# Small attention heads issued unit by unit instead of pair by pair

## The reference

```python
q = (hidden @ Wq + bq).reshape(...)
scores = einsum(q, k) * scale + mask
attn = softmax(scores)
out = einsum(attn, v) @ Wo + bo
```

## Time and profile before

| | us |
|---|---|
| three runs | 1409.1, 1414.52, 1415.49 |
| median | 1414.52 |
| the profiled execution, its own time | 1412.02 |
| its span, first to last instruction | 1410.7 |
| layer 0 and its MLP, about | 0 to 719 |
| layer 1, stream of heads | 719 to 849 |
| layer 2, stream of heads | 916 to 1119 |
| layer 3, stream of heads, and the last batch's end | 1181 to 1410.7 |

### The profile page before, as it was taken

The page is one execution under the profiler, slowest core; times in us unless marked ns, Lnnn a source line. Parts: engine busy times, 40 slices in busy tenths (PEclk is TensorE's granted clock), DMA queues, the critical chain, the costliest instruction groups (busy, mean ns, idle before and its releaser), DMA issues. The chain is left out here.

```text
span 1410.7 us, 26853 instructions
## 1 busy us (share of the span) xinstructions
PE 1289.9 (91%) x9901; PEld 1098.9 (78%) x9901; DVE 903.1 (64%) x2341; ACT 721.6 (51%) x1817; POOL 547.4 (39%) x1003
## 2 busy tenths in 40 slices
PE   7999999999999999998977787978888898999995
PEld 6999999999999999997865556855554587666663
DVE  6866767688856767687765657455556375465661
ACT  4866666677756666576214443235444522444442
POOL 3544544445444545453443325043323131223332
PEclk9999999999999999999986889968997798899997
DMA  5320000023200000022012101220120112011000
GB/s 166 105 69 1 2 1 5 2 68 112 62 2 1 2 1 1 1 71 92 24 47 72 48 2 46 69 77 25 50 70 1 50 42 79 17 37 56 13 3 16
DMA packets 44132, 56.69 MB, mean 40 GB/s; under 512 B 10016, under 2 KB 24416, under 8 KB 44000
## 3 DMA queue, kind: packets, MB, share of 16 engines
q1 hardware_dynamic: 38880, 54.40, 12.3%
q0 software_dynamic: 5120, 0.56, 0.3%
HBM read 32.68 MB, written 1.05 MB: 24 GB/s over the span
## 5 line engine op out<-in xcount | busy, mean ns | idle before, releaser
L1797 ACT ACTIVATE PT<-bank 128x512 f32<-128x512 f32 x320 | 174.2, 595 | 165.5 <-PE bank L1739 84.2
L1078 POOL TENSOR_SCALAR E<-E,rl 128x256 f32<-128x256 f32 x256 | 238.1, 941 | 0.0
L1903 POOL DMA_DIRECT2D Q<-rows x160 | 90.3, 566 | 216.4 <-ACT rows L1811 208.5
L1076 POOL TENSOR_TENSOR pb<-E,rl 128x2 f32<-128x2 f32 x128 | 33.7, 263 | 327.4 <-DVE rl L954 327.4
L821 ACT ACTIVATE QTh<-bank,bqs 128x256 fp32r<-128x256 f32 x128 | 60.7, 474 | 182.6 <-PE bank L117 182.6
L1861 DVE CUSTOM_DVE_ANT_0 Em<-bank,M 128x256 bf16<-128x256 f32 x256 | 95.2, 420 | 75.7 <-issue 45.5
L1854 DVE TENSOR_REDUCE nm<-bank 128x1 f32<-128x512 f32 x128 | 82.3, 685 | 74.2 <-PE bank L1708 73.7
L831 ACT ACTIVATE E<-bank,nm 128x257 f32<-128x257 f32 x256 | 119.3, 480 | 3.1 <-DVE nm L931 3.1
L938 DVE SCALAR_TENSOR_TENSOR QTl<-bank,bqs,QTh 128x256 fp32r<-128x256 f32 x128 | 61.8, 483 | 85.3 <-ACT KT L822 84.4
L1754 PE MATMUL bank<-PT,V 128*32 128x256 f32 x1280 | 103.7, 462 | 2.6 <-ACT PT L1797 2.6
L1731 PE MATMUL bank<-Q,K 51*128 51x256 f32 (+1 forms) x640 | 97.4, 319 | 6.3 <-ACT PT L1797 5.4
(11 more groups left out here) (465 smaller groups left out, 4505.5 us busy)
## 6 DMA issues: line engine op xcount, KB each, us to landing
stage<-in_wts SPq DMA_DIRECT2D x99, 256.0 KB, 3.1
Q<-stage SPq DMA_DIRECT2D x72, 128.0 KB
K<-stage SPq DMA_DIRECT2D x48, 128.0 KB
K<-xh SPq DMA_DIRECT2D x16, 128.0 KB, 2.9
Q<-rows POOLq DMA_DIRECT2D x96, 4.0 KB, 1.7
K<-stage SPq DMA_DIRECT2D x24, 64.0 KB
X<-in_x SPq DMA_DIRECT2D x4, 256.0 KB, 6.0
stage<-in_ctx SPq DMA_DIRECT2D x4, 256.0 KB, 3.6
```

Of the source, the lines that this page charges most:

```text
L1078: m = pool.tensor_scalar(s.E[:, i % 3, t, 0:256], s.E[:, i % 3, t, 0:256], s.rl[:, r, t:t + 1], None, ALU.mult)
L1797: act.activation(s.PT[i % s.NPT][:, 2 * u:2 * u + 2, :].rearrange("p a b -> p (a b)"), s.STB[y][:], ACT.Exp).then_inc(S["t_ex"])
L1903: pool.dma_start(f32(s.Q[b % s.NR][at:at + 2, pair:pair + n, :]), f32(s.rows[4 * n * y:4 * n * y + 4 * n, g % 2, :])).then_inc(S[f"dma_row ...
```

## The change

The loop of all engines runs over units n instead of pairs: a unit is one bank of scores, that is one head in layers 1 and 3 and half a head in layer 2 (`TB` units a batch: 16, 32, 32). In step n TensorE issues the scores by query of unit n and the scores by key of unit n - L, with L odd (13, 17, 13), matmul by matmul in turn, so that one is always on the even head's rows and the other on the odd head's. Both waits, for the maximum of unit n - 2 and the exponential of unit n - L - 2, stand ahead of the step. In layer 3 the two mask matmuls follow each unit.

The projections `q`, `k`, `k1` (now `x`), `v0`, `v1` and `c` are cut in two pieces of six matmuls, each in a step of its own (`k` of layer 3 stays whole); high and low parts are steps of their own one unit apart (`qh`, `ql`, `th`, `tl`, ...). `q_out` in layer 1 comes at step 11 of 16, all outputs in layer 2 at step 15 of 32. An attend is cut in two halves, in two consecutive steps. The steps after attention and the norms for the next MLP get tables by unit (`POSTS`, `NEXT_NORMS`). `TURN` sets when a group's maxima are turned (1 to 2 units after they are complete). The number of `PT` buffers is 8, 6, 8 instead of 6. In layer 1 the maxima and exponentials per unit are as before; no arithmetic changes. In VectorE's and ScalarE's loops the preparations come before the unit's maximum or exponential.

```diff
-DELAY = {1: 6, 2: 4, 3: 5}
+TURN = {1: 2, 2: 3, 3: 2}
+LAG = {1: 13, 2: 17, 3: 13}
+KEPT = {1: 8, 2: 6, 3: 8}
...
+IN_LAYER = {1: {0: ["mask", "k0", "stats"], 1: ["k1", "kh"], 2: ["kl", "norm"], 3: ["k_out", "maskrow"],
+                4: ["turn", "scale", "mask_out"], 5: ["v0", "th"], 6: ["v1", "va", "tl"], 8: ["q0"], 9: ["q1", "qh"],
+                10: ["ql"], 11: ["q_out"]},
+            2: {0: ["mask", "turn", "th"], 1: ["tl", "maskrow"], 3: ["q0"], 4: ["q1", "qh"], 5: ["ql"], 7: ["k0"],
+                8: ["k1", "kh"], 9: ["kl"], 11: ["x0"], 12: ["x1", "xh"], 13: ["xl"],
+                15: ["mask_out", "q_out", "k_out", "x_out"], 19: ["v0"], 20: ["v1", "va"], 23: ["v2"],
+                24: ["v3", "vb"]},
+            3: {0: ["mask", "turn", "th"], 1: ["tl"], 3: ["q0"], 4: ["q1", "qh"], 5: ["ql"], 7: ["k0", "kh"],
+                8: ["kl"], 12: ["q_out", "k_out"], 15: ["v0"], 16: ["v1", "va"], 19: ["maskparts"]}}
...
+POSTS = {1: [["po0", "on0"], ["po1", "on1"], ["onT", "oth"], ["otl"], ["c0"], ["c1", "y"]],
+         2: [["po0", "on0"], [], ["po1", "on1"], [], ["onT", "oth"], ["otl"], [], ["c0"], ["c1", "y"]],
+         3: [["po0", "on0"], ["po1", "on1"], ["po2", "on2"], ["po3", "on3"], ["onT", "oth"], ["otl"], ["c0"],
+             ["c1", "y"], ["fstats"], ["fnorm"]]}
...
+    def turns_at(self, n):
+
+        g, r = divmod(n - TURN[self.l] + 1, self.G * self.units)
+        return [g - 1] if r == 0 and 0 < g <= 2 * self.N // self.G else []
+
+    def attends_at(self, n):
+
+        g, k = divmod(n - self.L - 1, 4 * self.units)
+        half = self.nkt // 2
+        return [(g - 1, half * k + e) for e in range(half)] if 0 < g <= self.N // 2 and k < 2 else []
...
-    def scores(p, t):
...
+    def scores(n):
+
+        m = n - s.L
+        if n < s.T:
+            if n % s.TB == 0:
+                ready(n // s.TB)
+            if n < 2:
+                w.wait_ge(S["m_gelu"], 16 * l)
+            w.wait_ge(S["t_mx"], s.o["mx"] + (n - 1) * (2 if l == 3 else 1))
+        if 0 <= m < s.T:
+            p, u, y = s.unit(m)
+            g = 2 * p // s.G
+            w.wait_ge(S[f"dma_rows{g % 2}"], 32 * ((s.o["g"] + g) // 2 + 1))
+            w.wait_ge(S["t_ex"], s.o["ex"] + m - 1)
...
+        for e in range(2):
+            if n < s.T:
+                by_query(n, e)
+            if 0 <= m < s.T:
+                by_key(m, e)
+        if l == 3 and 0 <= m < s.T:
+            add_mask(m)
...
-    for p in range(s.steps()):
-        for u in range(s.units):
-            if p < s.N:
-                scores(p, u)
-            if 0 <= p - s.D < s.N:
-                weights_by_key(p - s.D, u)
-        for g in s.turns_at(p):
+    for n in range(s.steps()):
+        scores(n)
+        for g in s.turns_at(n):
             turn_maxima(g)
-        for gi in s.attends_at(p):
-            attend(gi)
-        b, steps = s.preps(p)
+        for gi, k in s.attends_at(n):
+            attend(gi, k)
+        b, steps = s.posts_at(n)
+        for x in steps:
+            heads_post_pe(c, s, b, x)
+        b, steps = s.preps(n)
         for x in steps:
             heads_prep_pe(c, s, b, x)
```

More of the change, by code:

```diff
@@ L1154, in __init__ @@
         self.N = NB * self.P
+        self.TB = 2 * self.P * self.units
+        self.T = NB * self.TB
         self.R = 3 * d + (0 if l == 3 else 1)
@@ L1742, in attend, with by_query @@
-    def attend(gi):
+    def by_query(n, e):
+        p, u, y = s.unit(n)
+        q, r = p % s.P, p // s.P % s.NR
+        at = slice(64 * y, 64 * y + s.R)
+        if l != 2:
+            z = pe.matmul(s.SB[y][:, 256 * e:256 * e + 256], s.Q[r][at, q, 128 * e:128 * e + 128],
+                          s.K[r][at, q // s.rp, :], start=True, stop=True)
+        elif e == 0:
+            z = pe.matmul(s.SB[y][:], s.Q[r][at, q, u * 128:u * 128 + 128], s.K[r][at, q, :], start=True, stop=True)
+        if e == (0 if l == 2 else 1):
+            z.then_inc(S["t_s"])
@@ new lines, in by_key, with add_mask @@
+    def by_key(n, e):
+        p, u, y = s.unit(n)
+        q, r = p % s.P, p // s.P % s.NR
+        at, o = slice(64 * y, 64 * y + s.R + 2), (2 * u + e) * 128
+        z = pe.matmul(s.STB[y][:, 256 * e:256 * e + 256], s.K[r][at, q // s.rp, o:o + 128], s.Q[r][at, q, :],
+                      start=l != 3 or e == 0, stop=l != 3, skip_group_check=l == 3)
+        if l != 3 and e == 1:
+            z.then_inc(S["t_st"])
+    def add_mask(n):
+        b, bank = n // s.TB, s.STB[n % 2]
+        pe.matmul(bank[:], s.identR[:], s.MTh[:, b % 2, :], start=False, stop=False, skip_group_check=True)
+        pe.matmul(bank[:], s.identR[:], s.MTl[:, b % 2, :], start=False, stop=True, skip_group_check=True
+                  ).then_inc(S["t_st"])
@@ L1743, in attend @@
+    def attend(gi, k):
         b, g = gi // (nh // 4), gi % (nh // 4)
@@ L1816, in heads_act @@
         act.copy(s.identR[:], c.ident[:]).then_inc(S["ident_r"])
-    for p in range(s.steps()):
-        b, steps = s.preps(p - 1)
+    for n in range(s.steps()):
+        b, steps = s.preps(n - 1)
         for x in steps:
             heads_prep_act(c, s, b, x)
-        b, steps = s.posts_at(p - 1)
+        b, steps = s.posts_at(n - 1)
         for x in steps:
             heads_post_act(c, s, b, x)
-        for b, x in s.norms(p - 1):
+        for b, x in s.norms(n - 1):
             if x == "parts":
```

350 lines of the change are left out of this document (152 added, 198 removed).

## The result

The kernel after takes **1509.2 us** (median of 4 runs, 1501.72 to 1522.42) against 1415.0 (4 runs): a ratio of 1.068, 95% interval 1.060 to 1.076. The forecast was 1400 in a range of 1368 to 1432, so it has the wrong sign, and the result lies 77 us above the upper end of its range. The profiled execution spans 1521.1 us, 110.4 more than before.

The account below looks back on a forecast made before the run. TensorE was taken to bound layer 3, a loop between engines layer 2, with layer 1 looser. Layers 1, 2 and 3 at +2, -23 and +10, and -1 for clock, turned 1412.0 into 1400 us, range 1368 to 1432.

Parts of the forecast that it names:

- Layer 3: +10 forecast: Layer 3, bound by TensorE: more passages between scores and masks or attends, less shorter waits, make it 10 us longer.
- six bare slots of 0.11: Layer 3, kernel before: a pair's eight score matmuls take 0.67 us, read as including six slots of 0.11.
- -1 for the clock: Whole kernel: the more even stream should lose less to the granted clock, a gain of 1 us.
- Rival B: Passages between tilings, mostly in layer 3, are dear; at 0.4 us each the kernel takes 1440. Chance 0.20.
- Layer 2: -23 forecast: Layer 2, paced by a loop between engines: stream 19 us shorter, end 4 shorter, together 23.
- what a unit's own matmuls take: Layer 2 stream: a unit's matmuls take about 0.25 us, leaving about 0.42 of its 0.68 for other work.
- my 50: Layer 2, sign of being right: VectorE waits under 50 us for scores, where it waited 65.8.
- Layer 1: +2 forecast: Layer 1: stream about +2 us by work, +3 by boundary waits, its end gives back 3; +2 in all.
- The wait for query DMAs: Layer 1, three batch boundaries: TensorE waits near 2.8 us at each for the query transfers, +3 us.
- Rival A: Whole kernel: TensorE is fed so evenly that it keeps full speed, giving 1374 us. Chance 0.22.
- Rival C: The faster stream runs into its transfers: three waits of about 4 us in layer 2 leave 1412. Chance 0.16.
- No cost: Joined waits: a late exponential also holds back scores by query; charged nothing, as ScalarE is busy half the stream.

Follow-up runs that it names:

- e6: Kernel after with one more full-array mask matmul (low part added a second time) behind each unit's masks in layer 3: 1477.7 us, ratio 1.045.
- e10: Kernel before with a third full-array mask matmul behind each of the 128 scores by key of layer 3: 1437.3 us, ratio 1.016.
- e13: Kernel before with layer 3's attends cut in two, the second half behind the next scores by query: 1421.2 us, ratio 1.005.
- e2: Kernel before with the odd head's scores by query moved between the two heads' masks in layer 3: 1491.8 us, ratio 1.055.
- e8: As e7 (only layer 2 by units), with each attend of layer 2 whole again: 1411.6 us, ratio 0.998.
- e11: Kernel after with, in layer 3, attends whole and the masks of two units issued together: 1460.3 us, ratio 1.032.
- e9: Kernel after with the attends of layer 3 whole again: 1437.3 us, ratio 1.013.
- e1: Kernel after with the masks of two units issued together after the second in layer 3: 1443.7 us, ratio 1.021.
- e7: Layer 2 by units as in the kernel after, layers 1 and 3 as in the kernel before: 1402.1 us, ratio 0.991.
- e3: Kernel after with layer 3 issuing both query matmuls of a unit, then both key matmuls: 1519.6 us, ratio 1.075.

## Why the prediction was wrong

**Layer 3: +10 forecast, +113 measured.** The sum of work was off by 13: a unit is 0.10 dearer than its 0.98 (128 x 0.10), which makes the +10 some +23, as the estimate above has it. The reason is a misreading of the earlier trace rows. I took the eight score matmuls, 0.67 us, for six bare slots of 0.11; they are four slots of two matmuls side by side. In the rows above the first takes 0.22 (1348.28 to 1348.50) and from the last one to the masks it is 0.21 (to 1348.71), which leaves 0.12 for each of the two between. So the sum credited the change with an overlap that the kernel before had, and left out the dearer first and last slot of every unit's scores. Two units take 2 x 1.08 = 2.16 us for a pair's 1.79, 0.37 more where I had 0.17.

The step that failed by most is one sentence: "I stay near the rows of warm, steady stretches, as the stream is meant to be steady", and the term that came of it, -1 for the clock. In layer 3 alone that term measured about +90. I had taken 0.96 in the earlier trace rows for a property of a busy layer; it was a property of that order of matmuls. In the kernel before, the clock of layer 3 too is low when the scores by key set in, and then rises and stays:

```profile
1197.50:1221.00 23.50, 23.47 (x142) 15.45 (x140) 10.94 (x58) 9.27 (x20) 5.32 (x15) 0.73 0.03 7
1222.00:1377.00 155.00, 151.32 (x1226) 99.49 (x1225) 95.17 (x480) 74.22 (x167) 52.60 (x124) 1.00 0.10 28
```

In the kernel after it rises only after 1300 and falls again (clock 1.00, then 0.50):

```profile
1305.00:1314.00 9.00, 9.00 (x69) 5.15 (x67) 5.61 (x26) 3.49 (x7) 2.53 (x8) 1.00 0.02 3
...
1332.00:1340.00 8.00, 8.00 (x35) 5.40 (x34) 1.78 (x9) 2.40 (x5) 0.39 (x2) 0.50 0.01 2
```

e6 and e10 show that the clock is the cause and not a companion: the same added work makes the layer 44 us shorter where the clock is low and 26 longer where it is high.

**Rival B** named the place and the direction: more passages, in the layer without slack. I gave it 0.20, and its price, 0.4 us each at half speed, came to 1440. It lacked the feedback: I priced passages at half speed but not the half speed of everything between them, which is the far larger part. At full speed a passage costs 0.23 us between scores and an attend (e13) and 0.37 between scores and masks (2.16 for 1.79), so the rival's point of decision, 0.30 each, lies between the two. What I cited from the Trainium skill, TensorEngine Tiling (Array Packing), section Key Properties, a drain at a change of mode, agrees with these prices in that there is one. The Trainium skill's page TensorE: Matmul & The Clock Gate, section A second HAM failure mode, tells of a kernel whose short pauses between groups of matmuls made its clock swing; the clock of layer 3 swings here too (0.50, 1.00 and 0.50 again in the rows above), but its rows show no pause, so that pauses are the reason is not shown.

**Layer 2: -23 forecast, -12.4 measured.** (Over eight profiles with this layer by units, otherwise unaltered, the median is 186.7, over four by pairs 199.5: -12.8.) The end was right: scores by key alone last 16.6 us for 21.6 (-5.0, forecast -4; from 1094.3 to 1115.9 before, from 1094.0 to 1110.6 after). The start costs 3.1 more (26.2 us to the first key scores for 23.1), since the lag is 17 units; I had allowed up to 2 a layer and put nothing in the sum. The stream took 144.3 for 154.8, -10.5, where -19 was forecast. The term that was mis-sized is what a unit's own matmuls take. At full speed, in rows of the two kinds of scores and a half attend:

```profile
964.39 0.50 PE L1734 MATMUL bank<-K,Q 49*128 49x512 f32 x1
...
964.83 1.07 PE L1793 MATMUL bank<-PT,V 128*32 128x256 f32 x16
965.83 0.49 PE L1734 MATMUL bank<-K,Q 49*128 49x512 f32 x1
```

Scores between two pieces take 0.44 us, not 0.25, and the half attend 1.00. So a unit with a piece is TensorE's, 1.44 long. Where a unit follows a piece and has none itself, its scores take 0.35 (965.83 to 966.18) and leave 0.68 - 0.35 = 0.33 for its neighbours' work, not 0.42. That is 0.1 to 0.2 of room less in each unit beside a piece, at most 32 x 0.19 = 6 us a batch, of which some was never to be used; the stream fell short by 8.5 in 3.5 batches, 2.4 a batch. It is the passage again, in a layer that I had taken to hide it; that it makes up the whole 2.4 is not shown. VectorE's wait came in under my 50: 43.6 in the window of the 65.8.

**Layer 1: +2 forecast, +1.5 measured, and right by luck.** The stream was to be 2 longer by its work and 3 by its waits, and is 8.8 shorter (80.0 for 88.8); the end was to give 3 back, and up to the last scores by key it is 7.4 longer (21.9 for 14.5), with 24.3 us at a clock of 0.50 for 17.4 at 0.90 over the stretches of the earlier trace rows; the start is 2.9 longer (26.6 for 23.7), where the sum had nothing. Over seven profiles with this layer by units it lasted 123.7 to 133.3 (median 130.6), over seven by pairs 126.1 to 130.5 (median 130.0), so the total is within its scatter. The wait for query DMAs came at each of the three boundaries, as forecast, but 1.7 to 1.8 us long and not 2.8:

```profile
753.26 0.55 PE L1731 MATMUL bank<-K,Q 49*128 49x256 f32 x1 [1.68 <-DMA Q<-stage]
776.47 0.35 PE L1731 MATMUL bank<-K,Q 49*128 49x256 f32 x1 [1.76 <-issue]
804.99 0.35 PE L1731 MATMUL bank<-K,Q 49*128 49x256 f32 x1 [1.78 <-issue]
```

The profile names the transfer at the first alone, but each time TensorE starts 2.2 to 2.5 us after SyncE has issued the last of the six query transfers (at 751.0, 774.1 and 802.5). The kernel before stood at two of its three boundaries, 1.89 and 1.78.

**Rival A** (full clock) is refuted outright: the streams of layers 1 and 2 stand at 0.84 and 0.85. **Rival C** has no sign: in layer 2 TensorE waits for no transfer, and in layer 1 5.2 us for 3.7. "No cost" for the joined waits held in layer 3: TensorE is idle 7.5 of 318 us in the kernel after, and in e6, which has the same waits, 3.0 of 164.7 at full speed.

**What stays open.** What tips the clock is not settled. The count of passages alone doesn't do it: in the kernel before 32 more left it at 0.94 (e13), while 59 more, with the odd query matmuls left without neighbours, took it to 0.76 (e2), and which of the two did it is not shown; in e8 and e11 whole attends went with a lower clock, in e9 with a higher one. Nor is it shown why a passage lowers the clock: that the array stands idle in it is inferred from e1, e6 and e9, since the rows count it as busy. And no run of the kernel after has its matmuls one by one, so against the overlap speaks the kernel before alone, whose rows show two score matmuls at a time too.

## What to carry to other kernels

Price a reordering of TensorE's work at both levels of its clock, and ask what holds the level that the rows show: a busy share of 98 or 100% doesn't. In the layer that TensorE bounds, keeping blocks of one tiling together gave back 81 us (e1) or 68 (e9), though both together less (58, e11); cutting pays in a stage where it has gaps, as in layer 2 here, and there alone the change is worth taking (e7, -0.9%). A cheap test for this cause is to add matmuls that bring no passage: if the stage gets shorter, it is the clock. And read in the trace whether an edit did what it was meant to do: e3 changed the order of issue and not what ran, and e2 changed more than its passage.

## What was not expected of the hardware

- TensorE busy 100.00 of 100 us by the rows at a granted clock of 0.50, twice as slow matmuls and no wait in sight.
- 128 added full-array matmuls made a layer 44 us shorter.
- The level persists in some orders: once e6 and the kernel before were at full speed, they stayed there for the rest of their streams (165 and 155 us), though the same matmuls had run at half speed for some 60 and 13 us at their start (71.3 us at 0.58, 23.5 at 0.73). The kernel after rose and fell again.
- In e3 matmuls on different rows of the array did not start in the order of issue: the first key matmul of a unit starts 0.37 us ahead of the second query matmul, which is issued before it.
